# A graph network's second and third pass made dense over all 100 node tiles

## The reference, cut to what matters

```python
h = jnp.maximum(_layernorm(x, axis=-1), 0.0)
# first layer
msg = node_feats[src] + edge_feats
agg = jax.ops.segment_sum(msg, dst, num_segments=n_nodes)
h = jax.nn.relu(agg @ W1 + b1) @ W2 + b2
h = (h - mean) * jax.lax.rsqrt(var + BN_EPS) * bn_gamma + bn_beta
# second layer, two times: x -> relu(conv(x)), with loops added once more
enorm = dis[src] * dis[dst]
xw = x @ W
out = jax.ops.segment_sum(xw[src] * enorm[:, None], dst, num_segments=n) + b
```

## Time and profile before

| | |
|---|---|
| median of 3 runs | 2981.77 us |
| profiled execution, first to last instruction (span; no other time of it is given) | 4462.9 us |
| mean granted TensorE clock | 0.809 |
| PE, VectorE, ACT, POOL busy in the span | 68%, 43%, 18%, 42% |
| dense matmuls (L1105) | 19200, 2378.8 us busy |
| gathers (L1266) | 1840 |
| chain that ended last | PE 51%, another core or an unknown queue 16%, VectorE 14%, issue 14% |

### The profile page before, as it was taken

The page is one execution under the profiler, slowest core; times in us unless marked ns, Lnnn a source line. Parts: engine busy times, 40 slices in busy tenths (PEclk is TensorE's granted clock), DMA queues, the critical chain, the costliest instruction groups (busy, mean ns, idle before and its releaser), DMA issues.

```text
span 4462.9 us, 66610 instructions
## 1 busy us (share of the span) xinstructions
PE 3021.2 (68%) x26545; PEld 2771.2 (62%) x26545; DVE 1930.8 (43%) x4856; ACT 795.8 (18%) x1708; POOL 1887.0 (42%) x1911
## 2 busy tenths in 40 slices
PE   1376666666766677737777777777857777777777
PEld 1265556666666566636667666666846766666667
DVE  9476667777777677742233332323301111111112
ACT  5122222222222223332111111111100000000000
POOL 6654444454454452033443344444144444444441
PEclk9987888888887788857787888887868878877788
DMA  4334333343434343343333333233453333333334
GB/s 118 84 101 110 98 100 112 97 116 101 115 100 114 96 116 104 111 125 120 113 100 113 113 112 130 88 129 115 149 127 127 112 122 118 113 124 113 112 128 124
DMA packets 341546, 504.30 MB, mean 113 GB/s; under 512 B 278786, under 2 KB 284344, under 8 KB 316401
## 3 DMA queue, kind: packets, MB, share of 16 engines
q1 hardware_dynamic: 280102, 402.60, 27.6%
q0 software_dynamic: 60512, 94.12, 9.8%
q10 hardware_dynamic: 616, 3.20, 0.3%
HBM read 362.65 MB, written 137.13 MB: 112 GB/s over the span
## 4 chain that ended last, share of the span: by engine, by line
PE 51%; another core or an unknown queue 16%; DVE 14%; issue 14%; ACT 2%; DVEq 1%; DMA 1%; SPq 0%; POOL 0%; ACTq 0%; POOLq 0%
PE psum L1105 34%; PE psum L1085 6%; DVE arena L958 4%; PE psum L1127 3%; PE psum L1120 3%; DVE arena L984 2%; DVE arena L955 2%; DVE arena L968 1%; PE psum L1068 1%; DVEq L1017 1%; ACT arena L1205 1%; PE psum L1140 1%; PE psum L1190 1%; PE psum L1186 1%
## 5 line engine op out<-in xcount | busy, mean ns | idle before, releaser
L1266 POOL DMA_INDIRECT arena<-table,srcT x1840 | 1799.8, 978 | 2248.8 <-PE psum L1127 1626.5
L1105 PE MATMUL psum<-arena 125*125 125x193 bf16 (+1 forms) x19200 | 2378.8, 274 | 385.6 <-issue 335.6
L1105 PEld LDWEIGHTS psum<-arena 125*125 125x125 fp8e4 x19200 | 2112.3, 157 | 491.6 <-issue 448.9
L1085 PE MATMUL psum<-arena 128*125 128x200 f16 x2272 | 609.4, 287 | 573.7 <-issue 290.0
L958 DVE TENSOR_SCALAR arena<-iota,keyT,oddT 128x200 f16<-128x200 f16 x2272 | 697.5, 335 | 601.3 <-remote 326.7
L1205 ACT CAST arena<-psum 125x400 uint16<-125x400 f32 x1136 | 548.8, 492 | 2131.8 <-PE psum L1085 1192.0
L1085 PEld LDWEIGHTS psum<-arena 128*125 128x125 f16 x2272 | 345.1, 157 | 660.5 <-issue 349.9
L955 DVE TENSOR_TENSOR arena<-modT,psum 128x500 f16<-128x500 f16 x568 | 376.3, 663 | 0.1
L1001 DVE TENSOR_REDUCE arena<-psum 125x64 f32<-125x192 f32 x192 | 67.2, 350 | 581.6 <-PE psum L1105 291.6
L968 DVE SCALAR_TENSOR_TENSOR arena<-relT,psum 128x960 bf16<-128x960 f16 x272 | 310.7, 1142 | 0.0
L984 DVE TENSOR_TENSOR arena<-arena 128x650 f32<-128x650 f32 (+1 forms) x334 | 274.4, 821 | 4.3 <-DMA arena<-in_edge_attr_dram 4.2
(11 more groups left out here) (217 smaller groups left out, 1037.0 us busy)
## 6 DMA issues: line engine op xcount, KB each, us to landing
arena<-counts SPq DMA_DIRECT2D x121, 1600.0 KB
counts<-arena SPq DMA_DIRECT2D x71, 1600.0 KB
arena<-in_edge_attr_dram SPq DMA_DIRECT2D x166, 320.0 KB
arena<-table,srcT POOLq DMA_INDIRECT x1840
table<-arena SPq DMA_DIRECT2D x8, 1050.0 KB
table<-arena SPq DMA_DIRECT2D x25, 168.0 KB
arena<-table SPq DMA_DIRECT2D x4, 1050.0 KB
arena<-in_x_dram ACTq DMA_DIRECT2D x4, 700.0 KB
```

What stands on the lines that cost most here:

```text
L1085: pe.matmul(to, ob(v // NB4 % NOB)[:, v % NB4, :], oh(v % NOH).rearrange("p (j m) -> p j m", m=2), start=True, stop=True).then_inc(p_bld, 1)
L1105: last = pe.matmul(ps_v[n % 2][0:PN, 0:xc], A(slot)[0:PN, j, 0:PN], Xs[0:PN, j, 0:xc], start=(j == 0), stop=(j == J - 1))
L1266: pool.indirect_dma_start(out=gbuf(slot)[0:parts, t, :], out_offset=None, in_=tables[k], in_offset=bass.IndirectOffsetOnAxis(ap=idx, axis= ...
```

## The change

- `DENSE` is (54, 100, 100). Passes 2 and 3 sum all 100 tiles with count matrices; they have no groups and no gathers. Pass 1 stays at 54 tiles and 79 gathered groups.
- Pass 2 builds 48 matrices (52 to 99) and fetches 52; pass 3 fetches 100. In pass 2's plan a built tile stands at about every second place from the seventh on, and its runs are spread over one step between two such tiles (at most 64 units).
- Runs have `SUB = 5` nodes, 25 to a tile. A one-hot has 300 columns (source tile x 3 words). Two neighbouring runs write five words of a bank, where the middle word is shared: the second matmul adds to it (`start` only for the first). 13 evictions to a tile, of 500 columns, the last of 300. A run on the odd side has its node numbers moved by one half word ("side").
- A comparison serves five runs (625 columns), `NOB = 2`, `NOH = 7`. `modT` is uint8. 2550 runs in 20 columns of 128 for 2272 in 18.
- Preparation has a few operations more (`sub`, `side`, a second `is_ge`) and fewer elsewhere (`tile_p`, `four`), and its buffers lie in `acc`.

```diff
-SUB = 4
-NSUB = 32
+SUB = 5
+NSUB = 25
+NWORD = 5
 NAP = 25
 XC = 3 * F + 2
 AP_STEP = 4
 NSLOT = 4
 NEDGE = 2
 NS = 2
-NOH = 6
-NB4 = 4
-NOB = 3
+NOH = 7
+NB4 = 5
+NOB = 2
 NA = 4
 NBANK = 2
 TURN_GAP = 2.6
-DENSE = (54, 69, 69)
+DENSE = (54, 100, 100)
...
-        n_b = 0
+        n_b, step = 0, NAP * (D - 7) / max(1, len(built) - 1)
         for q in range(D):
-            if n_b < len(built) and q >= 6 and (q - 5) * len(built) >= n_b * (D - 7):
+            if n_b < len(built) and (q - 6) * (len(built) - 1) >= n_b * (D - 7):
                 seq.append(("built", built[n_b]))
                 n_b += 1
             else:
                 seq.append(("loaded", old.pop(0)))
         assert not old and n_b == len(built)
+        span = min(step, 3 * NAP - 11)
+    n_b = 0
...
-                    t = start[q] - 3 * NAP + 2 + i * (3 * NAP - 11) / NSUB
+                    t = start[6] - 9 + n_b * step - span + i * span / NSUB
                 pe.append((t, "bld", b))
-                if i % 2:
+                if i % 2 or i == NSUB - 1:
...
+            n_b += 1
...
-    QG = [(PN * d * (E // N) - MARGIN) // (P * NT) for d in DENSE]
+    QG = [(PN * d * (E // N) - MARGIN) // (P * NT) if d < J else NG for d in DENSE]
+    EC = [min(q * P * NT, E) for q in QG]
     G0 = QG[0]
-    KC = J * SUB // 2
+    KC = J * (SUB + 1) // 2
+    NEV = (NSUB + 1) // 2
...
             V(dve.tensor_scalar(rel, rel, 0.0, SUB - 1.0, ALU.max, ALU.min))
+            V(dve.tensor_tensor(by_run(rel), by_run(rel), per_run(run_f[:, 5, :], c0, c1), ALU.add))
             V(dve.tensor_scalar(upper, rel, 2.0, None, ALU.is_ge))
+            V(dve.scalar_tensor_tensor(out=upper, in0=rel, scalar=4.0, in1=upper, op0=ALU.is_ge, op1=ALU.add))
             dve.scalar_tensor_tensor(out=odd, in0=upper, scalar=-2.0, in1=rel, op0=ALU.mult, op1=ALU.add).then_inc(
                 v_odd, 1)
...
-            V(dve.scalar_tensor_tensor(out=flo, in0=flo, scalar=SUB / 2.0, in1=upper, op0=ALU.mult, op1=ALU.add))
+            V(dve.scalar_tensor_tensor(out=flo, in0=flo, scalar=(SUB + 1) / 2.0, in1=upper, op0=ALU.mult, op1=ALU.add))
...
-                    V(dve.tensor_scalar(bad[0:1, 1:2], ps_s[0:1, 0:1], SCALE * QG[k] * EG, None, ALU.is_equal))
+                    V(dve.tensor_scalar(bad[0:1, 1:2], ps_s[0:1, 0:1], SCALE * EC[k], None, ALU.is_equal))
...
-                    pair, s = v // 2, v % 2
-                    if s == 0 and pair >= NBANK:
+                    i = v % NSUB
+                    pair, side = v // NSUB * NEV + i // 2, i % 2
+                    if side == 0 and pair >= NBANK:
                         pe.wait_ge(a_ev, pair - NBANK + 1)
                     if k == 1 and v == pl["b"]:
                         pe.wait_ge(a_loop, NL)
-                    to = ps_b[pair % NBANK][0:PN, :].rearrange("p (j s m) -> p j s m", s=2, m=2)[:, :, s, :]
-                    pe.matmul(to, ob(v // NB4 % NOB)[:, v % NB4, :], oh(v % NOH).rearrange("p (j m) -> p j m", m=2), start=True,
-                              stop=True).then_inc(p_bld, 1)
+                    to = ps_b[pair % NBANK][0:PN, :].rearrange("p (j m) -> p j m", m=NWORD)
+                    pe.matmul(to[:, :, 2 * side:2 * side + 3], ob(v // NB4 % NOB)[:, v % NB4, :],
+                              oh(v % NOH).rearrange("p (j m) -> p j m", m=3), start=(side == 0),
+                              stop=(side == 1 or i == NSUB - 1), skip_group_check=True).then_inc(p_bld, 1)
...
-                    act.copy(A2(slot)[0:PN, :, i // 2 * SUB:(i // 2 + 1) * SUB],
-                             ps_b[b // 2 % NBANK][0:PN, :].rearrange("p (j x) -> p j x", x=SUB)).then_inc(a_ev, 1)
+                    n_w, at = NWORD if i % 2 else 3, b // NSUB * NEV + i // 2
+                    act.copy(A2(slot)[0:PN, :, i // 2 * NWORD:i // 2 * NWORD + n_w],
+                             ps_b[at % NBANK][0:PN, :].rearrange("p (j x) -> p j x", x=NWORD)[:, :, 0:n_w]).then_inc(
+                                 a_ev, 1)
```

More of the change, by code:

```diff
@@ L303, in bass_gnn_preln_kernel @@
         psum = ctx.enter_context(nc.psum_tensor("psum", [P, 8, 512], F32))
-        ps_b = [psum[:, i, 0:2 * KC] for i in range(NBANK)]
+        ps_b = [psum[:, i, 0:J * NWORD] for i in range(NBANK)]
         ps_v = [psum[:, i, 0:3 * F + 1] for i in (4, 7)]
@@ L462, in bass_gnn_preln_kernel @@
         rel_c = fl
-        iota_s = part(o_t + 2 * NE, 0, NE // 2).bitcast(F16)
+        iota_s = acc[:, 3 * NE:o_late].bitcast(F16)
         less = [part(o_t, i, NE // 2).bitcast(BF16) for i in range(2)]
@@ L466, in bass_gnn_preln_kernel @@
         iota_si = part(o_t, 0, NE).bitcast(I32)
[L467 to L478, removed]
+        odd_h, mod_h = iota_s, rel_r.bitcast(F16)[:, 0:NE]
+        o_r = o_late
+        iota = acc[:, o_r:o_r + P]
+        run_f = acc[:, o_r + P:o_r + P + 6 * NC].rearrange("p (i c) -> p i c", c=NC)
+        run_i = acc[:, o_r + P + 6 * NC:o_r + P + 7 * NC].bitcast(I32)
+        run_b = acc[:, o_r + P + 7 * NC:o_r + P + 8 * NC].bitcast(I32)
+        o_f = o_r + P + 8 * NC
+        first_f = acc[:, o_f:o_f + NRB].rearrange("p (i c) -> p i c", c=NRB)
+        run_first = acc[:, o_f + NRB:o_f + 2 * NRB].bitcast(I32)
+        o_n = o_f + 2 * NRB
+        less_m, scale_b = (acc[0:PN, o_n + i * J:o_n + (i + 1) * J] for i in range(2))
+        assert o_n + 2 * J == n_late and o_t + 2 * NE <= o_v
         halves = [(0, 8), (8, NC)]
@@ L580, in dve_late_constants @@
                                        op0=ALU.mult, op1=ALU.add))
-            V(dve.tensor_scalar(limit, late, float((QG[1] - QG[0]) * EG), float(QG[0] * EG), ALU.mult, ALU.add))
+            V(dve.tensor_scalar(limit, late, float(EC[1] - EC[0]), float(EC[0]), ALU.mult, ALU.add))
+            sub, side = run_f[:, 4, :], run_f[:, 5, :]
+            V(dve.tensor_scalar(sub, bound, 1.0 / PN, 0.5 / PN - 0.5, ALU.mult, ALU.add))
+            V(dve.tensor_scalar(sub, sub, MAGIC, None, ALU.add))
+            V(dve.tensor_scalar(sub, sub, MAGIC, None, ALU.subtract))
+            V(dve.scalar_tensor_tensor(out=sub, in0=sub, scalar=-float(PN), in1=bound, op0=ALU.mult, op1=ALU.add))
+            V(dve.tensor_scalar(side, sub, 0.5 / SUB, 0.25 / SUB - 0.5, ALU.mult, ALU.add))
+            V(dve.tensor_scalar(side, side, MAGIC, None, ALU.add))
+            V(dve.tensor_scalar(side, side, MAGIC, None, ALU.subtract))
+            V(dve.scalar_tensor_tensor(out=side, in0=side, scalar=-2.0 * SUB, in1=sub, op0=ALU.mult, op1=ALU.add))
+            V(dve.tensor_scalar(side, side, 1.0 / SUB, None, ALU.mult))
         def dve_first_rows():
-            node, tile, four = (first_f[:, i, :] for i in range(3))
+            node = first_f[:, 0, :]
             dve.wait_ge(l_first, 16)
             V(dve.tensor_copy(node, run_first))
[L589 to L596, removed]
+            V(dve.tensor_scalar(node, node, 1.0 / SUB, 0.5 / SUB - 0.5, ALU.mult, ALU.add))
+            V(dve.tensor_scalar(node, node, MAGIC, None, ALU.add))
+            V(dve.tensor_scalar(node, node, MAGIC, None, ALU.subtract))
             V(dve.tensor_scalar(node, node, 0.5 - SEED, None, ALU.add))
@@ L618, in dve_rows @@
             V(dve.tensor_scalar(row, ps_rw, -1.0, 0.0, ALU.add, ALU.max))
+            V(dve.tensor_scalar(row, row, float(NROW - 1), None, ALU.min))
             dve.tensor_copy(run_i, row).then_inc(v_row, 1)
```

38 lines of the change are left out of this document (17 added, 21 removed).

## The result

The changed kernel takes 3462.39 us (median of 4 runs, 3454.76 to 3466.0) against 2982.14 us (4 runs, 2980.24 to 2989.39) for the kernel before: a ratio of 1.1597, 95% interval 1.1575 to 1.162. It is 480 us slower. The forecast was 3400 us with a range of 3300 to 3480: right in sign and in range, 62 us low and 18 us from the range's upper end. The span that it gave for the profile of the changed kernel, 3850 us and shorter than the one before, was wrong: that span is 3462.5 us.

A forecast was written before the change was run, and what follows sets the result against it. The prediction took VectorE to bound pass 1, PE pass 2, PE and POOL together pass 3. Terms -105 + 12 + 332 + 205 = +444, less 25 of waits, +419 on 2981.77: 3400 us, range 3300 to 3480.

The forecast's parts named there:

- the sum of unstopped stretches: Whole kernel before: pass work without stops, plus the head and the gap between passes, gives 2774 of 2982 us.
- the 208 us left over: Rest of the 2982 us median, left for two ends of pass, the tail and all waits.
- the page with 3850 us: Profile of the changed kernel: span near 3850 us, below 4462.9, so the page would show a faster kernel.
- rival D: Stops in passes 2 and 3 are in the runs too; the changed kernel takes 2570 us; chance 0.03.
- Head, +12: Ahead of pass 1: four more indirect DMAs and more, longer passes over the keys cost 12 us.
- Pass 1, -105: Pass 1, VectorE: one-hots -56 and comparisons -60 make -116, less 11 for PE and POOL close behind.
- So VectorE still ends last: Pass 1 after the change: VectorE 1085 us, against PE 930 and POOL 978 from 782 gathers at 1.25.
- Pass 2, +332: Pass 2, PE: 31 more tiles +270, builds +112, groups -50; VectorE and ACT covered.
- by columns: 0.134: Pass 2, PE: a 300-column build priced at 0.134 us from the 200-column one; 1200 builds add 112 us.
- Pass 3 and its waits, +205 - 25: Pass 3, PE: tiles +266, groups -50, POOL's excess -11; some 25 us of gather waits in passes 2 and 3 go.
- B: Pass 1 gives nothing, as PE and VectorE pace each other or wide one-hots cost by columns: 3505 us; chance 0.11.
- C: Gathers slow the unprofiled kernel too; 100 to 150 us come back in passes 2 and 3: 3250 to 3300; chance 0.11.

The follow-up runs named there:

- e8: The kernel before, unchanged, profiled on a chip without stops: 2983.33 us, span 2981.9.
- e1: The kernel before, unchanged, profiled a second time, on the chip with stops: 4471.19 us, beside 4462.9 for its partners without a profile.
- e10: The changed kernel without pass 1's gathers but for four groups, on a chip without stops: 3389.0 us, against 3460 to 3465 for the changed kernel.
- e6: Runs of five with DENSE (58, 69, 69), four more dense tiles in pass 1 than (54, 69, 69): 2936.09 us, ratio 0.9832 to the kernel before.
- e11: The changed kernel with each build writing its 300 PSUM columns in one stretch, not three words of every five, counts wrong: 3417.72 us.
- e13: The changed kernel with one-hots made from numbers in PSUM (f32), not SBUF (f16), on a chip without stops: 3680.62 us.

## Why the prediction was right, and where it failed

- **Which of the two times to use.** I took the sum of unstopped stretches, 2774 us of 2982, and charged the change by those steps. As a base for differences that held: in e8 the passes take 1313, 742 and 681 us where the working had 1201, 721 and 656, so 158 of the 208 us left over lie inside the passes, 112 of them in pass 1. The reason I gave failed: the profiler doesn't make the stops, they are in the runs of that chip too (e1). So did what followed from it, the page with 3850 us. Had the timed runs been on the chip with stops, the forecast of +419 would have been wrong by my own estimate above; rival D, the stops in the runs as well, is true there and nowhere else here.
- **Head, +12.** Measured +11.
- **Pass 1, -105.** Measured -88. The VectorE terms are right: one-hots 0.268 us apart (predicted 268 ns), comparisons 0.715 (predicted 715), VectorE's busy time 1214 to 1096, -118 for -116. The failed step is "So VectorE still ends last", with gathers at 1.25 us each: they take 1.47, the wider one-hots among the reasons, and POOL ends last in most of the pass. Removing them frees 76 us (e10); trading some of them for builds frees nothing (e6), so the others are close behind.
- **Pass 2, +332.** Measured +373; the largest miss. The mis-sized term is the build "by columns: 0.134": it takes 0.156 to 0.157. 1200 x 0.023 = 28 of the 41 us. e11 shows what I left out: 0.13 is the price of 300 columns in a row, and writing three words of every five costs the rest. It costs the two matmuls behind each build 16 us as well, which covers the other 13. The build of 200 columns writes with gaps too, two words of every four, and its 0.09 is by columns the price in a row; so it isn't gaps as such, and the nearest row couldn't show it. Why three of five is dear stays open. That VectorE and ACT are covered held: PE is busy 1112.95 of 1115.
- **Pass 3 and its waits, +205 - 25.** Pass 3 measured +204, the gap ahead of it -16, together +188 for +180. Row by row: 885 us where I had 868 and the ends of the pass.

```profile
2700.00:2800.00 100.00, 100.00 (x1189) 100.00 (x1188) 8.96 (x30) 2.41 (x9) 0.00 (x0) 1.00 0.52 189
```

100.00 of 100 busy and 1189 matmuls, against 643 in the same length of the earlier trace rows; a tile of 100 with its turn takes 8.47 us in most cases (median of 99). The transfers stayed hidden, at 52% of the engines for 189 GB/s.

- **Rivals.** B (pass 1 gives nothing) is out by -88, though its reason, three engines near each other, is there: POOL's gathers ended last, and the pass gained 17 us less than forecast. C, 100 to 150 us coming back in passes 2 and 3, is out: only 16 us and the excess of POOL came back.

Nothing large was saved by another term: of the 62 us, pass 1 is 17, pass 2 41 and the rest together 4.

In e8, POOL's gathers and their issue are 85% of pass 3's chain (2276:2957):

```profile
by line: POOL arena L1266 64.0%; issue 20.8%; PE psum L1105 11.8%; DMA arena<-table,srcT 1.2%; PE psum L1127 1.0%; PE psum L1068 0.7%; DVEq L1017 0.2%; PE psum L1190 0.1%; PE psum L1186 0.1%; DVE acc L1019 0.1%; DVEq L1019 0.0%
```

532 x 1.25 = 665 of 681 us. So the gathers did bound that pass, as the working said, but PE stood close behind, busy 664.85 us. Taking them away frees next to nothing when every group of 10 gathered matmuls becomes 57 dense ones: 31 tiles are 3100 matmuls in place of 532.

## What to carry to other kernels

A move that takes work from one full engine and gives it to another full engine is priced by the receiver: dense tiles cost PE 8.5 us each and freed POOL time behind which PE was just as full. When the profile's span and the timed median differ by half, compare the same program on several chips before using any share of the profile; sums over stretches in which an engine is full carry over, shares of the span don't. And price an operation by its access pattern, not its column count alone, and gathers by what VectorE does at the same time.

## What the runs showed of the hardware that was not expected

- On one chip of four the same program took 4463 us for 2983, by stops of PE, VectorE and ACT that come with gathers (POOL goes on issuing them), some 0.75 us each (0.38 in one kernel). The cause is open, and so is whether it is the chip or the time at which it was used.
- A gather's 0.94 us grows beside VectorE operations that read SBUF: to 1.044 on average beside 300-column f16 one-hots, 0.957 beside 200-column ones, 1.33 to 1.47 beside f32 additions of two SBUF tiles, 3.23 in the place shown. Beside one-hots that read PSUM it doesn't (390 gathers in e13). For the additions this is a reading of overlaps.
- A 300-column one-hot with two scalars costs 0.268 us from SBUF in f16, and 0.498 from PSUM in f32.
- A 300-column matmul into three PSUM words of every five holds PE 0.156 us, in a row 0.13, and slows the two matmuls behind it by 13 ns together. A 200-column one into two words of every four takes 0.09, no more by columns than in a row.
